# A two-layer graph network with residual and layer norm: the main loop rebuilt on a ring of four PSUM pairs

## The reference, cut to what matters

```
def sage(x, W_l, b, W_r):
    agg  = segment_sum(x[src], dst, 100000)
    mean = agg / max(deg, 1)
    return mean @ W_l + b + x @ W_r
h = relu(sage(x, W1_l, b1, W1_r))
h = relu(sage(h, W2_l, b2, W2_r))
out = layernorm(x + h @ W3 + b3)        # over the 256 features, no gain
```

## Time and profile before

| what | us |
|---|---|
| median of 3 runs | 3318.33 (3307.94 to 3328.46) |
| profiled execution, first to last instruction | 3317.4 |
| first to last `xdb` of the 49 passes | 45.0 to 2576.3 |
| busy: TensorE / VectorE / ScalarE / GpSimd | 2928.3 / 2695.7 / 1899.9 / 2689.2 |

### The profile page before, as it was taken

How to read it: one execution, slowest core, us unless ns; L and a number is a source line. 1 busy time by engine, 2 the same in 40 slices (tenths; PEclk the granted TensorE clock), 3 DMA queues, 4 the chain that set the end, 5 groups by cost and what they waited for, 6 DMA issues and landing times. The chain is left out here.

```text
span 3317.4 us, 57863 instructions
## 1 busy us (share of the span) xinstructions
PE 2928.3 (88%) x18433; PEld 2638.2 (80%) x18433; DVE 2695.7 (81%) x5026; ACT 1899.9 (57%) x3188; POOL 2689.2 (81%) x2614
## 2 busy tenths in 40 slices
PE   6999898999998998999989999999989698787876
PEld 5888887888887888888878888888878687676775
DVE  5778788877888788888988988888888787777775
ACT  4656555556665555655555656556555465555654
POOL 5888888888888888888888888888888767777776
PEclk9999999999999999999999999999999898898988
DMA  3444434434443434434344343444434455555553
GB/s 114 140 145 133 151 128 139 139 127 148 137 139 133 144 130 144 139 127 158 133 142 143 132 157 125 142 142 143 139 127 158 164 199 188 166 201 186 175 191 120
DMA packets 253118, 488.23 MB, mean 147 GB/s; under 512 B 37615, under 2 KB 165206, under 8 KB 253090
## 3 DMA queue, kind: packets, MB, share of 16 engines
q1 hardware_dynamic: 202498, 387.58, 34.2%
q0 software_dynamic: 50176, 99.91, 9.9%
q10 hardware_dynamic: 416, 0.40, 0.0%
HBM read 284.67 MB, written 206.22 MB: 148 GB/s over the span
## 5 line engine op out<-in xcount | busy, mean ns | idle before, releaser
L908 PE MATMUL ps_y<-w_hi,h_hi 128*128 128x256 f32 x1960 | 584.3, 298 | 180.4 <-DVE h_lo L683 180.1
L683 DVE TENSOR_TENSOR h_lo<-h_full,h_hi 128x512 fp32r<-128x512 f32 x784 | 712.3, 946 | 34.3 <-ACT h_hi L511 24.8
L384 POOL TENSOR_SCALAR o<-y,rs,nb 128x256 f32<-128x256 f32 x784 | 659.7, 850 | 1.7 <-DMA out_dram<-o 1.7
L509 ACT ACTIVATE h_full<-ps_h,bias 128x512 f32<-128x512 f32 x784 | 538.3, 687 | 197.1 <-PE ps_h L897 169.5
L908 PE MATMUL ps_y<-w_lo,h_hi 128*128 128x256 f32 x1960 | 572.5, 292 | 0.0
L908 PE MATMUL ps_y<-w_hi,h_lo 128*128 128x256 f32 x1960 | 572.5, 292 | 0.0
L342 POOL DMA_INDIRECT xe<-in_x_dram,e_stage x392 | 412.7, 1053 | 177.2 <-issue 94.8
L908 PEld LDWEIGHTS ps_y<-w_hi,h_hi 128*128 128x128 f32 x1960 | 396.6, 202 | 200.0 <-issue 189.1
L503 ACT CAST xt_hi<-ps_x 128x512 fp32r<-128x512 f32 x392 | 210.9, 590 | 596.1 <-PE ps_x L887 596.1
L669 DVE TENSOR_TENSOR xt_lo<-ps_x,xt_hi 128x512 fp32r<-128x512 f32 x392 | 252.7, 686 | 334.2 <-ACT xt_hi L503 334.0
L396 POOL TENSOR_TENSOR xb<-xn,b_row 128x1024 f32<-128x1024 f32 x196 | 477.1, 2434 | 35.7 <-DVE nb L719 32.2
(11 more groups left out here) (121 smaller groups left out, 7054.1 us busy)
## 6 DMA issues: line engine op xcount, KB each, us to landing
xn<-in_x_dram SPq DMA_DIRECT2D x196, 512.0 KB, 6.6
out_dram<-o SPq DMA_DIRECT2D x196, 512.0 KB
seg<-seg_tab SPq DMA_DIRECT2D x74, 512.0 KB, 4.6
xdb_tab<-xdb SPq DMA_DIRECT2D x49, 512.0 KB, 3.9
h_tab<-src_h SPq DMA_DIRECT2D x49, 512.0 KB
h_tab<-dst_h SPq DMA_DIRECT2D x49, 512.0 KB
xn<-h_tab SPq DMA_DIRECT2D x49, 512.0 KB, 5.2
xb<-xdb_tab SPq DMA_DIRECT2D x49, 512.0 KB, 4.1
```

The costliest lines, as they stand in the source:

```text
L384: ins = nc.gpsimd.tensor_scalar(o[:, b, s], y[:, b, s], rs[:, b, s:s + 1], nb[:, b, s:s + 1], ALU.mult, ALU.add)
L509: nc.scalar.activation(h_full[:, n, k], ps_h[n][:, k], ACT.Relu, bias=bias[:, n, k:k + 1]).then_inc(hf_ok[n], 1)
L683: nc.vector.tensor_tensor(h_lo[:, n, k], h_full[:, n, k], h_hi[:, n, k].bitcast(f32), ALU.subtract).then_inc(hlo_ok[n], 1)
L908: ins = nc.tensor.matmul(ps[:, s // 2, s % 2 * D:(s % 2 + 1) * D], a[:, k, s * P:(s + 1) * P], wx[:, w, k], start=first, stop=end)
```

## The change

The four PSUM pairs lose their fixed roles and form a ring, `pair[0..3]`. Pair `g % 4` holds in turn the first layer of g, the turned x of g+2, the second layer of g, and later the third layer of g; in between the edge work of step g+2 uses it. TensorE's order in a step becomes: turn of g+2, first layer of g+1, edge work, third layer of g-1, second layer of g. So three groups are in flight.
- `high_x`, `low_x`, `low_h`, the cast of `high_h`, `residual`, and the edge adds are one instruction of 1024 wide instead of two of 512; the relus stay 512 wide. `h_hi` and `h_lo` get a third buffer.
- `xe_full` and its four 512-wide copies go: cast, subtraction and scan read PSUM.
- `normalise` moves from GpSimd to ScalarE (four activations of 256 wide with scale and bias per row).
- On VectorE the `moments` come before `low_h(g, 1)`.
- SP stores group g-2 in step g (before: g-4), and loads x for g+4 in step g; the order of edge stores shifts, and `seg` is loaded at `u` = 0.
- In the edge stage the residual is one 1024-wide instruction; the rest is renamed.

```diff
-            def normalise(b):
-                for s in range(S):
-                    ins = nc.gpsimd.tensor_scalar(o[:, b, s], y[:, b, s], rs[:, b, s:s + 1], nb[:, b, s:s + 1], ALU.mult, ALU.add)
-                ins.then_inc(o_ok, 1)
...
+            def high_x(g, b, ps):
+                act.wait_ge(xt_ps, (g + 1) * K)
+                nc.scalar.copy(xt_hi[:, b], ps[:, :, :]).then_inc(xhi_ok, 1)
+            def high_h(g, n, h, ps):
                 for k in range(K):
                     act.wait_ge(l_ps[n], g * K + k + 1)
+                    after(act, hlo_ok[n], g)
+                    nc.scalar.activation(h_full[:, n, k], ps[:, k], ACT.Relu, bias=bias[:, n, k:k + 1]).then_inc(hf_ok[n], 1)
+                act.wait_ge(hf_ok[n], (g + 1) * K)
+                nc.scalar.copy(h_hi[:, h], h_full[:, n]).then_inc(hhi_ok[n], 1)
...
+            def normalise(g, b):
+                act.wait_ge(nb_ok, g + 1)
+                after(act, y_out[b], 8 * (g - b))
+                for s in range(S):
+                    ins = nc.scalar.activation(o[:, b, s], y[:, b, s], ACT.Identity, bias=nb[:, b, s:s + 1], scale=rs[:, b, s:s + 1])
+                ins.then_inc(o_ok, 1)
...
@@ ScalarE, step g = 4i + u @@
+                    high_x(g + 2, u % 2, pair[u])
+                    deviation(g - 2, u % 2)
+                    high_h(g + 1, 0, (u + 1) % 2, pair[(u + 1) % 4])
+                    edges(i, u, pair[(u + 2) % 4])
+                    normalise(g - 2, u % 2)
+                    high_h(g, 1, 2, pair[u])
...
@@ VectorE, step g @@
+                    low_x(g + 2, u % 2, pair[u])
+                    factors_rows(g - 2, u % 2)
+                    low_h(g + 1, 0, (u + 1) % 2)
+                    edges(i, u, pair[(u + 2) % 4])
+                    residual_rows(g - 1, (u + 1) % 2, pair[(u + 3) % 4])
+                    moments_rows(g - 1, (u + 1) % 2)
+                    low_h(g, 1, 2)
...
@@ VectorE, edges at u == 0 @@
+                    dve.wait_ge(xshi_ok, i + 1)
+                    nc.vector.tensor_tensor(xe_lo[:, 0], ps[:, :, :], xe_hi[:, 0].bitcast(f32), ALU.subtract).then_inc(xs_ok, 1)
+                    dve.wait_ge(seg_in, 16 * (i + 1))
+                        nc.vector.tensor_tensor_scan(run[:, k], seg[:, 0], ps[:, k], run[:, k, G - 1:G], ALU.mult, ALU.add)
...
@@ TensorE, step g; edges_left waits at u == 1 for xs_ok and run_ok, at 0, 2, 3 for dst_ok, xd_ok, src_ok @@
+                        pe.wait_ge(hf_ok[0], (g + 1) * K)
+                        turn_rows(i + (u + 2) // U, (u + 2) % U, pair[u])
+                        pe.wait_ge(xlo_ok, g + 2)
+                        edges_left(i, u)
+                        first_layer((u + 1) % 2, pair[(u + 1) % 4])
+                    after(pe, y_ok, g - 1)
+                    edges(i, u, pair[(u + 2) % 4])
+                        third_layer(g - 1, pair[(u + 3) % 4])
+                    pe.wait_ge(hlo_ok[0], g + 1)
+                        pe.wait_ge(xlo_ok, g + 3)
+                    second_layer(u % 2, pair[u])
...
@@ SP, step g @@
+                        sp.wait_ge(xt_ps, (g + 1) * K)
+                        sp.wait_ge(xb_ok, g + 1)
+                        sp.dma_start(xn[:, u], rows(x, g + U)).then_inc(x_in[u], 16)
@@ u == 0: seg, edge_store(i - 1, 3); u == 1: edge_store(i, 0); u == 3: edge_store(i, 2) @@
+                        store(g - 2, u % 2)
```

More of the change, by code:

```diff
@@ L547, in _ @@
             act.wait_ge(fill_out, 16)
+            high_h(0, 0, 0, pair[0])
+            high_x(1, 1, pair[3])
             def body(i, first, last):
@@ L678, in _, with residual @@
             dve.wait_ge(cleared, 7)
[L680 to L685, removed]
-                for k in range(K):
-                    dve.wait_ge(l3, g * K + k + 1)
-                    nc.vector.tensor_tensor(y[:, b, 2 * k:2 * k + 2].rearrange("p s d -> p (s d)"), ps_y[:, k],
-                                            xb[:, b, 2 * k:2 * k + 2].rearrange("p s d -> p (s d)"), ALU.add).then_inc(y_s, 1)
+            low_h(0, 0, 0)
+            low_x(1, 1, pair[3])
+            def residual(g, b, l3, y_s, ps):
+                dve.wait_ge(l3, (g + 1) * K)
+                nc.vector.tensor_tensor(y[:, b].rearrange("p s d -> p (s d)"), ps[:, :, :].rearrange("p k g -> p (k g)"),
+                                        xb[:, b].rearrange("p s d -> p (s d)"), ALU.add).then_inc(y_s, 1)
             def moments(g, b, y_s, stats_s, mv_s):
@@ L980, in body @@
                     g = i * U + u
-                    pe.wait_ge(xlo_ok, (g + 1) * K)
-                    after(pe, hf_ok[0], g * K)
-                    for m in range(K):
-                        columns([(X1R, xt_hi[:, u % 2], xt_lo[:, u % 2])], ps_h1, m).then_inc(l_ps[0], 1)
-                    edges(i, u)
-                    if not (first and u == 0):
-                        last_layer(g - 1, 1, hlo_ok[1], y_ok, l3_ps)
-                    if not (last and u == U - 1):
-                        ps_x_free(i, u)
-                        turn_rows(i + (u + 1) // U, (u + 1) % U, g + 1)
@@ L991, in body @@
-                    if first and u == 0:
-                        pe.wait_ge(w_ok, 2)
-                        pe.wait_ge(idx_ok, 6)
-                        pe.wait_ge(prep, PREP_RDEG)
-                    pe.wait_ge(hlo_ok[0], (g + 1) * K)
-                    after(pe, hf_ok[1], g * K)
-                    for m in range(K):
-                        columns([(X2R, h_hi[:, 0], h_lo[:, 0])], ps_h2, m).then_inc(l_ps[1], 1)
+                    if not (last and u >= 2):
+                        pe.wait_ge(hf_ok[0], (g + 1) * K)
+                        turn_rows(i + (u + 2) // U, (u + 2) % U, pair[u])
```

276 lines of the change are left out of this document (121 added, 155 removed).

## The result

| | before | after |
|---|---|---|
| median, us | 3313.14 (3303.72 to 3328.46, 4 runs) | 3069.99 (3069.12 to 3071.51, 4 runs) |
| after / before | | 0.9259, 95% interval 0.9231 to 0.9287 |
| profiled span, us | 3317.4 | 3068.0 |
| main loop, us a pass | 52.7 | 47.45 |
| busy a pass from 45 to 2300 us, VectorE / ScalarE / GpSimd, us | 44.2 / 30.9 / 44.7 | 39.5 / 34.0 / 35.6 |

What follows compares the result with a forecast made beforehand. TensorE and GpSimd were taken to set the pace together. A pass of 46.2 + 1.9 = 48.1 us gave -225 us; 3317.4 - 225 + 5 = 3097.4, with 0.9 to the median 3098; range 3005 to 3250.

Steps and rivals of the forecast that it cites:

- Bound: Main loop before: TensorE and GpSimd together set the pace, 52.7 us a pass, 6.5 of it lost by TensorE.
- The floor of 46.2: TensorE in the main loop: a pass without a gap takes 46.2 us.
- Waits of TensorE: Main loop after: third layer waits 0.2 at `u` = 0, scans 0.1, third layer 1.2 at `u` = 1; 1.5 a pass.
- Clock: TensorE's granted clock after: gaps mostly cost none; 0.4 us a pass added for growing ones, one in four at 1.6.
- Work: Engine sums per pass after: VectorE 38.0 us plus collisions, ScalarE 36, GpSimd about 36.
- Start, boundary: Start and boundary: GpSimd's shorter lists about -2, ScalarE's last normalise about +2.5; taken as 0, bounds -5 and +5.
- a wait on `seg` loads: Sign named in advance that would show the forecast wrong; no size given.
- Edge stage: Edge stage: the 1024-wide residual ends about 0.5 us later each time; between 0 and 25, taken as +5 us.
- Never waits: Rival, 7%: collisions too rare to matter, pass 46.2 to 46.6 us, total 2999 to 3019.
- The slower rival: Rival, 9%: at `u` = 1 first and third layers both stall, clock falls; pass 54.2 us, total 3392.
- The wait in the queue: Rival, 7%: SP's store waits for normalise with loads behind it, 1.5 us lost per step; within 1%, 3318.
- Width: VectorE: one 1024-wide instruction saves 0.07 us a pair by the rows, 0.157 by the skill's formula; off the path.

Runs made afterwards that it cites:

- b_no_lock: Kernel before, normalise still on GpSimd, with GpSimd's adds xb and xdb cut to 64 of 1024 columns; 3036.29 us, 0.9106 of before.
- b_norm_act: Kernel before with only normalise moved from GpSimd to ScalarE, ahead of the cast of the next x; 3552.16 us, 1.0688 of before.
- b_norm_no_lock: b_norm_act with GpSimd's adds xb and xdb cut to 64 of 1024 columns; 3174.46 us, 0.9550 of before.
- b_norm_late: Kernel before with normalise moved to the end of ScalarE's step, behind the second layer's casts; 3378.21 us, 1.0118 of before.
- a_no_lock: Kernel after with GpSimd's adds xb and xdb cut to 64 of 1024 columns; 3024.44 us, 0.9103 of before.
- a_moments_last3: Kernel after with low_h(g, 1) put back ahead of the moments on VectorE; 3217.79 us, 0.9728 of before.
- a_norm_pool: Kernel after with normalise put back on GpSimd in its old place; 3382.29 us, 1.0174 of before.
- a_root_later: a_moments_last3 with ScalarE's root and VectorE's factors also put behind the next first layer's high and low part; 3113.77 us, 0.9373 of before.

## Why the prediction was right, step by step

- **Bound.** "TensorE and GpSimd together set the pace" is half wrong. The collisions set it (b_no_lock; b_norm_act against b_norm_no_lock); that GpSimd's list alone did not, b_norm_late makes likely. The floor of 46.2 held: a_no_lock runs at 46.6 and b_no_lock at 46.8.
- **Waits of TensorE.** Forecast 0.2 at `u` = 0, 0.1 for the scans, 1.2 at `u` = 1; measured 0.28, none, 0.80. The mechanism, places and order were right. The last term was taken from the upper part of its own 0.7 to 1.4; the low end was the right one, because `low_h`, behind the moments, met only the last 0.7 us of `xb` and took 1.79.
- **Clock.** Forecast 0.4 a pass, measured 0 (granted clock 1.00). The waits, 1.1 instead of 1.5, and the clock are 0.8 too much; 0.15 a pass that I can't place goes the other way: 48.1 against 47.45.
- **Work.** VectorE 38.0 and collisions; busy 36.1 where there are none (a_no_lock), so 1.9 too much, and 39.5 with them. I had added durations of 1.22, while back to back the wide operations start 1.14 apart. ScalarE 36, busy 34.0. GpSimd 36, busy 35.6, and that was luck: I took a heavy pass's 17.5 from a full list of 53, where the average is 13.5 from 44.7, which leaves 31. The missing 4 came back as longer index copies and DMA issues on GpSimd (`e_stage`, 128x4: median 178 ns before, 1186 after; `xe` issues 1053 and 1277 on average).
- **Start, boundary.** Forecast 0 with 5 either way, measured +4.3. The named sign "a wait on `seg` loads" does appear once: the first scan of the edge stage waits 5.64 us for `seg`. The second starts 11.7 after the memset, against 12.2 before, so it is made up there. **Edge stage.** Forecast +5, measured 0; why is open.
- **Sum of the misses.** Main loop -253.6 instead of -225, so -28.6; start and boundary +4.3; edge stage -5: -29.3, against 3068.0 - 3097.4 = -29.4.
- **Rivals.** "Never waits" is what a_no_lock shows, 3024. The slower rival needed VectorE 2 us later; a_moments_last3 shows its first half, the wait for the scans, and there the clock did fall. The wait in the queue is what a_norm_pool shows. The lock itself first by the rows: `low_h` ran 1.1 us past the end of `xdb`, while the moments and the scan with a PSUM operand ran unhindered beside `xb` and `xdb`. The Trainium skill, page "SBUF — State Buffer", section "SBUF: two separate sides", says that whichever starts second fully blocks, and limits this, outside the 2-port modes, to a VectorE operation with two SBUF inputs; for `low_h` the trace agrees, and with the limit too. My price from it, up to 12 us a pass on VectorE, was over three times too high (3.4): it took every GpSimd tensor operation to catch something at full length, but only those count that meet an operation with two SBUF operands.
- **Width.** The rows' 0.07 a pair was right (1.27 to 1.29 against 1.21 to 1.22). The Trainium skill, page "VectorE: DVE Perf Modes", in its section on the TRN2 errata, gives (N + 151) / 0.96 ns, from which my estimate of 0.157 a pair followed. For one operation the traces agree (0.685 at 512, 1.22 at 1024); for two back to back they don't.

What stays open: how the gain is to be shared between the ring and the new order of VectorE and GpSimd, since no kernel with the new order and two groups in flight was run; what a shorter GpSimd list alone is worth; and why the boundary takes 3.3 us longer.

## What to carry to other kernels

When an operation's worst time is several times its median, look at what runs beside it before moving work between engines: here two GpSimd adds of 2.4 us, together five operations a pass, cost some 300 us (b_no_lock, 0.9106), and moving 13.5 us a pass off GpSimd alone made the kernel slower. Ask of each moved operation what its engine's queue holds behind it while it waits, and of each unloaded engine what it will now start earlier and beside what. A wait that is taken away can come back one step on, so read the wait of the next step too.

## What the runs showed of the hardware

- Beside a GpSimd tensor_tensor that started first, VectorE's operation with two SBUF tensors is held to its end (`low_h` 2.65 instead of 1.2; two scans 4.56 instead of 2.5). With one operand in PSUM it isn't (scans 2.44 beside `xdb`), nor are row statistics (1.41 beside `xb`).
- The other way round GpSimd is held too: in the kernel after, its 128x4 copy `e_stage` behind `xb` takes 1.19 us while the caught `low_h` runs (1197.21 to 1198.40; `low_h` ends at 1198.35), where it took 0.18 before.
- GpSimd's tensor_scalar of 128x256 lasts 0.55 us. Four in a row beside VectorE's `low_h` and `mean` took 4.13 instead of 2.2, and `mean` 1.52 instead of 1.21 (a_norm_pool).
- Idle times of TensorE of 0.3 and 0.8 us in a pass, or one of 1.3 (a_root_later), left the granted clock of the main loop at 1.00; with 2.0 once a pass it was 0.99 from 45 to 1200 us and 0.98 from 1200 to 2300 (a_moments_last3).
